# Cross-attention scores: the transposed scores computed a second time on TensorE, or turned by transposes after GpSimd has subtracted the row maximum

## The reference

```python
# L0 cross-attention, 16 heads of 8 features, query x, key and value ctx
q, k, v = proj(x, wq, bq), proj(ctx, wk, bk), proj(ctx, wv, bv)      # (B, 16, 256, 8)
scores = einsum('bhqd,bhkd->bhqk', q, k) / sqrt(8)
scores = where(mask[:, None], scores, -1e9)
attn = softmax(scores, axis=-1)
x = einsum('bhqk,bhkd->bhqd', attn, v)                               # then wo, bo
# L0 memory, ahead of it (w1, b1, w2, b2 updated by one gradient step)
out_mem = silu(x_in @ w1.T + b1) @ w2.T + b2
out = sigmoid(out_swa @ lin1.T) * out_swa + sigmoid(out_mem @ lin2.T) * out_mem
# L0 ffn, behind it: top 2 of 8 experts with a capacity; each token's row is scattered to its two experts
```

## Time and profile before

| | us |
|---|---|
| median of 3 runs (range) | 1086.91 (1083.47 to 1094.82) |
| the profiled execution | 1093.54 |
| its span, first to last instruction | 1091.5 |
| phase two: scores of step 0 begin | 342.64 |
| scores of steps 1, 2, 3 begin | 418.97, 497.19, 571.97 |
| last slots of step 3 written | 638.66 |

### The profile page before, as it was taken

The page is one execution under the profiler, slowest core; times in us unless marked ns, Lnnn a source line. Parts: engine busy times, 40 slices in busy tenths (PEclk is TensorE's granted clock), DMA queues, the critical chain, the costliest instruction groups (busy, mean ns, idle before and its releaser), DMA issues.

```text
span 1091.5 us, 14695 instructions
## 1 busy us (share of the span) xinstructions
PE 767.9 (70%) x4586; PEld 496.2 (45%) x4586; DVE 529.8 (49%) x1947; ACT 393.6 (36%) x924; POOL 158.9 (15%) x207
## 2 busy tenths in 40 slices
PE   5888787968453986977968919992664664664664
PEld 4445353544121663653645617882442442442442
DVE  4244253443333945936939321112556556556556
ACT  3514434252111542533532513330343343343343
POOL 9200000000101004013012040002040040040020
PEclk8798998999566997997977959997887887887886
DMA  7400000000106035054040011311000010010000
GB/s 220 144 7 13 1 19 0 19 0 0 53 22 103 2 54 93 0 64 81 9 64 20 2 43 37 91 49 44 20 25 6 29 24 5 29 24 5 10 0 10
DMA packets 49236, 39.37 MB, mean 36 GB/s; under 512 B 11234, under 2 KB 42658, under 8 KB 49188
## 3 DMA queue, kind: packets, MB, share of 16 engines
q1 hardware_dynamic: 47140, 34.62, 14.7%
q0 software_dynamic: 2048, 4.20, 1.4%
HBM read 27.20 MB, written 11.60 MB: 36 GB/s over the span
## 4 chain that ended last, share of the span: by engine, by line
PE 52%; DVE 20%; issue 11%; ACT 8%; DMA 5%; POOL 2%; SPq 2%; DVEq 0%; POOLq 0%; ACTq 0%
PE bank L1219 4%; DMA q_stack<-parts_dram 4%; PE bank L1208 4%; DVE R L2066 2%; PE bank L1102 2%; PE bank L960 2%; PE bank L1105 2%; PE bank L1104 2%; PE bank L1115 2%; PE bank L892 2%; PE bank L1022 2%; PE bank L1074 2%; PE bank L1029 2%; PE bank L1298 2%; PE bank L983 2%
## 5 line engine op out<-in xcount | busy, mean ns | idle before, releaser
L1815 DVE CUSTOM_DVE_ANT_0 bank<-bank,add_q 128x256 f32<-128x256 f32 x256 | 100.2, 458 | 45.2 <-PE bank L1074 29.6
L1509 ACT ACTIVATE pT<-bank 128x512 f32<-128x512 f32 x128 | 76.1, 597 | 73.7 <-PE bank L1105 71.4
L1074 PE MATMUL bank<-k_stack,q_stack 96*128 96x256 bf16 x256 | 52.1, 303 | 40.0 <-DMA q_stack<-parts_dram 34.8
L1238 PE MATMUL bank<-ident,X 128*128 128x128 f32 x48 | 14.3, 420 | 89.7 <-DVE X L1923 89.7
L1102 PE MATMUL bank<-q_stack,k_stack 96*128 96x256 bf16 x256 | 70.4, 275 | 2.1 <-DVE mx L1815 2.1
L1104 PE MATMUL bank<-add_k,ident_b 128*128 128x256 bf16 x256 | 70.8, 276 | 0.0
L1105 PE MATMUL bank<-neg_max,head_sel 96*128 96x256 bf16 x256 | 70.7, 276 | 0.0
L1298 PE MATMUL bank<-XT,kpad 128*128 128x256 f32 (+1 forms) x256 | 59.1, 364 | 3.3 <-DVE cT L2023 3.2
L2023 DVE TENSOR_TENSOR cT<-bank,decay 128x384 f32<-128x384 f32 x64 | 35.7, 558 | 43.8 <-POOL decay L847 43.3
L1298 PEld LDWEIGHTS bank<-XT,kpad 128*128 128x128 f32 x256 | 47.9, 210 | 16.5 <-DVE cT L2023 9.5
L1074 PEld LDWEIGHTS bank<-k_stack,q_stack 96*128 96x128 bf16 x256 | 25.3, 105 | 64.8 <-DMA q_stack<-parts_dram 31.8
(11 more groups left out here) (401 smaller groups left out, 1775.0 us busy)
## 6 DMA issues: line engine op xcount, KB each, us to landing
k_stack<-parts_dram SPq DMA_DIRECT2D x48, 64.0 KB
q_stack<-parts_dram SPq DMA_DIRECT2D x24, 128.0 KB, 10.1
expert_in<-no_rows SPq DMA_DIRECT2D x8, 324.0 KB, 3.9
rows<-expert_in SPq DMA_DIRECT2D x8, 324.0 KB
expert_out<-rows_y SPq DMA_DIRECT2D x8, 324.0 KB
moe_w<-in_L_ffn_w_dram SPq DMA_DIRECT2D x1, 2048.0 KB
parts_dram<-k_parts SPq DMA_DIRECT2D x4, 384.0 KB, 2.7
parts_dram<-q_parts SPq DMA_DIRECT2D x12, 128.0 KB, 1.7
```

Source lines behind the costliest of these rows:

```text
L1074: last = pe.matmul(q_bank(n)[:, c * S:(c + 1) * S], q_stack[:, h // 2, b * S + c * P:b * S + (c + 1) * P], k_stack[:, h // 2, h % 2, b * S ...
L1509: act.activation(pT[:, g % 2, j], k_bank(n)[:].rearrange("p (c q) -> p c q", c=QC), ACT.Exp).then_inc(exp_ready.sem, 1)
L1815: last = dve.tensor_tensor_reduce(sc, sc, add_q[:, b * QC + c, :], 1.0, 2.0 * NEG, ALU.add, ALU.max, mx[:, c, h:h + 1])
```

## The change

Each unit now has its scores on TensorE once. VectorE's reduction writes scores plus mask to an SBUF ring `shifted` (SLIDE = 4 units deep) and the two maxima to `mx`. GpSimd subtracts the maxima from the unit's 128x512 elements with one instruction (`s_shifted`). TensorE then transposes the four 128x128 blocks to PSUM (`scores_T`), and ScalarE takes the Exp as before. `scores` runs LEAD = 3 units in front. `mask_k`, `add_k`, `neg_max`, `maxima_T` and `negated` are gone. Silu is now half of z (1 + tanh(z/2)): Tanh and Identity on ScalarE, one VectorE instruction for the product, and the half goes into `memT`. `stack` is cut in `stack_k` and `stack_q`: for step 0 the K half is loaded ahead of `save_q`, and later steps wait for the last `s_ready` in place of `sT_ready`. The 8 scatters of a step move to the next step's units 2, 5, ..., 23. `outputs_T` of each batch is cut in two.

```diff
-        masks_loaded = signal("masks_loaded", 32)
+        masks_loaded = signal("masks_loaded", 16)
-        AHEAD = 14
+        LEAD = 3
+        SLIDE = 4
+        s_shifted = signal("s_shifted", XU)
...
+        z_of = (g2[:], memT[:])
+        mx = sb("mx", [P, SLIDE, QC], scope=stage)
+        shifted = sb("shifted", [P, SLIDE, QC, S], scope=stage)
...
+        pe_at = {3: 0, 5: 1, 7: 2, 9: 3, 11: 4, 13: 5, 15: 6, 18: 7, 23: 8, 25: 9}
+        act_at = {3: 0, 5: 1, 7: 2, 9: 3, 11: 4, 15: 6, 21: 7, 23: 8}
+        dve_at = {7: 0, 9: 1, 11: 2, 13: 3, 15: 4, 17: 5, 19: 6, 22: 7, 25: 8, 28: 9}
+        o_at = {21: 0, 23: 1}
...
             save_k(0)
+            stack_k(0)
             save_q(0)
-            stack(0)
+            stack_q(0)
...
-                    sp.wait_ge(*sT_ready.at(i))
-                    stack(i + 1)
+                    sp.wait_ge(*s_ready.at(i))
+                    stack_k(i + 1)
+                    stack_q(i + 1)
...
+            def scatter(i, n):
+
+                if n == 0:
+                    wait_apart(pool, passed, *slots_ready.at(i))
+                pool.indirect_dma_start(expert_in, bass.IndirectOffsetOnAxis(slot_i[:, n:n + 1], 0), Xm[:, n % NC, :], None).then_inc(scattered.sem, 16)
+
+            def heads(i, following):
+                for n in range(XU):
+                    wait_apart(pool, passed, *s_read.at(i, n + 1))
+                    pool.tensor_tensor(shifted[:, n % SLIDE], shifted[:, n % SLIDE], mx[:, n % SLIDE].unsqueeze(2).to_broadcast([P, QC, S]), ALU.subtract).then_inc(s_shifted.sem, 1)
+                    if following and n == 4:
+                        split_k(i + 1)
+                    if not is_first(i) and n % 3 == 2 and n // 3 < PAIRS:
+                        scatter(i - 1, n // 3)
                 if following:
+                    masks(i + 1)
...
-                def scores_k(n):
...
+                def scores_T(n):
+
+                    pe.wait_ge(*s_shifted.at(i, n + 1))
+                    if n >= 2:
+                        pe.wait_ge(*exp_ready.at(i, n - 1))
                     for c in range(QC):
+                        for k in range(QC):
+                            last = pe.transpose(sT_bank(n)[:, k * S + c * P:k * S + (c + 1) * P], shifted[:, n % SLIDE, c, k * P:(k + 1) * P], ident[:])
                     last.then_inc(sT_ready.sem, 1)
...
+                for n in range(LEAD):
+                    scores(n)
+                for n in range(XU):
+                    if n + LEAD < XU:
+                        scores(n + LEAD)
+                    scores_T(n)
+                    if n >= 5 and n % 4 == 1:
+                        values((n // 4 - 1) // G, (n // 4 - 1) % G)
+                    if n in o_at:
+                        outputs_T(0, o_at[n])
+                    if following and n == 1:
+                        keys(i + 1)
+                    if following and n in pe_at:
+                        head(i + 1, pe_at[n])
...
                     act.wait_ge(*zT_b.at(i, n + 1))
-                    act.activation(hT[:, n, 0:T], bank[1][:], ACT.Silu, bias=b1_new[:, n:n + 1]).then_inc(hT_b.sem, 1)
+                    if n >= 2:
+                        act.wait_ge(*hT_b.at(i, n - 1))
+                    act.activation(hT[:, n, 0:T], bank[1][:], ACT.Tanh, bias=b1_half[:, n:n + 1], scale=0.5)
+                    act.activation(z_of[n % 2], bank[1][:], ACT.Identity, bias=b1_new[:, n:n + 1]).then_inc(z_act.sem, 1)
...
+                if n < FC:
+                    dve.wait_ge(*z_act.at(i, n + 1))
+                    dve.scalar_tensor_tensor(hT[:, n, 0:T], hT[:, n, 0:T], 1.0, z_of[n % 2], ALU.add, ALU.mult).then_inc(hT_b.sem, 1)
...
                     wait_apart(dve, passed, *s_ready.at(i, n + 1))
+                    if n >= SLIDE:
+                        wait_apart(dve, passed, *sT_ready.at(i, n - SLIDE + 1))
                     for c in range(QC):
-                        last = dve.tensor_tensor_reduce(sc, sc, add_q[:, b * QC + c, :], 1.0,
-                                                        2.0 * NEG, ALU.add, ALU.max, mx[:, c, h:h + 1])
+                        last = dve.tensor_tensor_reduce(shifted[:, n % SLIDE, c, :], q_bank(n)[:, c * S:(c + 1) * S], add_q[:, b * QC + c, :], 1.0,
+                                                        2.0 * NEG, ALU.add, ALU.max, mx[:, n % SLIDE, c:c + 1])
```

More of the change, by code:

```diff
@@ L822, in _ @@
             pool.wait_ge(*slots_zero.at(0))
-            with pool.Fori(0, STEPS - 1) as i:
-                mix(i, True)
-            mix(STEPS - 1, False)
+            heads(0, True)
+            with pool.Fori(0, STEPS - 2) as i:
+                tail(i, True)
+                heads(i + 1, True)
+            tail(STEPS - 2, True)
+            heads(STEPS - 1, False)
+            tail(STEPS - 1, False)
+            for n in range(PAIRS):
+                scatter(STEPS - 1, n)
             pool.wait_ge(*scattered.at(STEPS - 1))
@@ L1139, in mix @@
-                pe.wait_ge(*slots_ready.before(i))
-                for g in range(NB * G + 1):
-                    for n in range(4 * g, min(4 * g + 4, XU)):
-                        scores_k(n)
-                        ahead = n + AHEAD
-                        if ahead < XU:
-                            scores_q(ahead)
-                        if ahead % 8 == 1 and ahead <= XU + 1:
-                            maxima_T(ahead // 8 - 1)
-                        if following and n in later:
-                            head(i + 1, later[n])
-                    if g == 6:
-                        outputs_T(0)
-                    if g > 0:
-                        values((g - 1) // G, (g - 1) % G)
@@ L1155, in mix @@
+                values(NB - 1, G - 1)
+                for c in range(QC):
+                    outputs_T(1, c)
                 if following:
-                    pe.wait_ge(*exp_ready.at(i))
+                    pe.wait_ge(*s_read.at(i))
+                    pe.wait_ge(*pv_ready.at(i))
                     values_of(i + 1)
@@ L1817, in mix @@
                     last.then_inc(s_read.sem, 1)
[L1819 to L1836 removed]
+                    if n - LEAD - 1 in o_at:
+                        outputs_of(0, o_at[n - LEAD - 1])
@@ L1837, in mix @@
+                    if following and n in dve_at:
+                        head(i + 1, dve_at[n], head_chain)
+                for c in range(QC):
+                    outputs_of(1, c)
                 if following:
@@ L2074, in _ @@
             head_chain = Chain(dve, dve_h, 0)
-            for n in range(4, 10):
+            for n in range(10):
                 head(0, n, head_chain)
```

166 lines of the change are left out of this document (52 added, 114 removed).

## The result

The changed kernel takes 1098.3 us (median of 20 runs, 1088.2 to 1106.8) against 1088.8 us (20 runs, 1081.6 to 1094.8): ratio 1.0074, 95% interval 1.0049 to 1.0100. Forecast were 1089.5 us and a range of 1068 to 1113. The time is inside, 8.8 us above the forecast; the medians differ by 9.5 us, where 2.6 were forecast.

What follows compares the result with a forecast made beforehand. TensorE was taken to bound the units, GpSimd to bound steps 1 to 3 after the change. The terms -6.2 - 4.9 + 18.5 + 4.6 - 7.4 - 0.4 - 1.6 = +2.6 us gave 1089.5 us, range 1068 to 1113.

Steps and rivals of the forecast that it cites:

- to the first reduction: Ahead of step 0: K's loads issued early save time, a second ScalarE instruction per MLP chunk costs 2.7 us; together -6.2 us.
- step 0: First of phase two's four steps: TensorE stays the bound, 47.9 us plus 2.1 of coupling, 50.0 us: -4.9.
- step 1, step 2: Middle steps of phase two: GpSimd becomes the bound with 51.7 us of work and 6.0 of stalls, 60.3 us: +9.2, +9.3.
- step 3: Last step of phase two: GpSimd's 48.6 us of work set it, with 1 us of stalls, 52.2 us: +4.6.
- turns to steps 1, 2: Between steps: stacks load earlier and VectorE's late start regains 3.7 of 7.4 us, twice: -7.4, plus 0.4 per tail.
- turn to step 3, last tail: Into step 3 the turn gains only 0.4 us; tail transposes cut in two gain 0.4 a step.
- The subtract: GpSimd's 32 subtracts of 128x512 a step: 1.20 us each from start to start, between 1.04 and 1.50.
- The stalls between engines: Waits within steps: 6.0 us in steps 1 and 2 (2.5 at unit 13, 2 low clock, 1.5 coupling), 2.1 in step 0.
- The fast subtract: Rival, chance 0.27: GpSimd isn't the wall, the subtract takes 1.04 us, stalls are 2 instead of 6 us; about 1070 us.
- The slow one: Rival, chance 0.14: the subtract takes 1.50 us and adds 29 us in steps 1 to 3, about 4 in step 0; 1122 us.
- TensorE's clock: Rival, chance 0.12: TensorE, partly idle in each unit, falls to its low clock, so a unit takes 1.8 us; 1112 us.
- The fourth rival: Chance 0.12: 9 VectorE instructions with two SBUF inputs keep GpSimd's subtracts waiting, 6.2 us a step in three steps; 1104 us.

Runs made afterwards that it cites:

- e11: Kernel before the change, with k_stack's first loads issued ahead of Q's first saves and VectorE's loop over the steps written out: 1073.5 us, ratio 0.9849.
- e3: Changed kernel with VectorE's split of Q moved from unit 28 to behind the last reduction: 1101.8 us, ratio 1.0103 to the kernel before.
- e7: Changed kernel with the split of Q behind the last reduction and k_stack's loads issued ahead of Q's saves: 1083.3 us, ratio 0.9948 to the kernel before.
- e5: Changed kernel without GpSimd's subtracts of the row maximum; transposes wait for the reductions instead: 1059.0 us, ratio 0.9718 to the kernel before.
- e9: As e7, with VectorE's loop over steps 0 to 2 written out: 1070.3 us, ratio 0.9836 to the kernel before.
- e10: As e11, with k_stack loaded in two halves, the first batch's as soon as unit 15 has used it: 1072.7 us, ratio 0.9856 to the kernel before.
- e1: Changed kernel with all 8 scatters of a step issued ahead of the next step's first subtract: 1104.0 us, ratio 1.0113 to the kernel before.
- e2: Changed kernel with 4 scatters ahead of the first subtract, the rest behind units 14, 17, 20, 23: 1096.9 us, ratio 1.0064 to the kernel before.
- e4: Changed kernel with TensorE's other blocks ahead of each unit's four transposes, not behind them: 1099.1 us, ratio 1.0090 to the kernel before.

## Why the prediction was right, and where it was wrong

| term | forecast | measured | |
|---|---|---|---|
| to the first reduction | -6.2 | -7.2 | right |
| step 0 | -4.9 | +3.2 | wrong sign |
| step 1, step 2 | +9.2, +9.3 | +9.3, +10.4 | right size, wrong sum |
| step 3 | +4.6 | -2.9 | wrong sign |
| turns to steps 1, 2 | -4.1, -4.1 | -4.3, -4.9 | right |
| turn to step 3, last tail | -0.8, -0.4 | +2.0, -1.0 | clock |
| sum in phase two | +2.6 | +4.6 | |

(The forecast's 0.4 us for each tail stands with its turn.) Outside phase two come the 3.0 us that the two turns of the second layer cost, a term that was put at nothing; the rest of the medians' 9.5 us is not accounted for. By the sign that the prediction itself named it was wrong, since the subtract is off its 1.20 us by more than 0.1. That the time came out near is in good part luck.

**Ahead of step 0.** The second instruction on ScalarE goes with 2.3 us (Q is saved 39.3 us behind the key projection, 37.0 before), forecast 2.7. From the save to the scores it takes 10.6 us; Q's half was put at 2 + 9. e11, without ScalarE's part, shows K first by itself: -10.8.

**The subtract** was taken at 1.20 us from start to start and runs at 1.0: the near end of the bracket, the flat row's 1.04. The per-partition broadcast and a different second operand cost nothing here. So the forecast had 6.4 us a step too much here.

**The stalls between engines** are the step that failed. I gave TensorE's bound in step 0 a coupling of 2.1 us and GpSimd's in steps 1 and 2 stalls of 6.0. With 1.0 us a subtract GpSimd's list in step 1 is 32.0 + 3.1 + 10.2 + 0.95 + 1.6 = 47.9 us, and the step took 60.4: 12.5 us of stalls. In step 0 TensorE was busy 48.0 us and idle 10.0. The forecast had it busy 51.5 - 7.0 = 44.5; its 47.9 holds 3.4 us of waits. A broken-up queue makes TensorE busier by itself: four transposes take 0.66 us after a wait and 0.44 in a row (the chain above). Steps 1 and 2 came out right because 6.4 too much stood against 6.5 too little. Scores, reduction, subtract and transposes form a ring with three units of lead, and each engine also carries blocks of 1 to 4 us (`split_k`, the MLP product, the split of Q). I priced one such meeting (2.5 us at unit 13) and rounded the rest. e3 and e7 measured another: the split of Q at unit 28 costs 2.4 to 3.5 us a step in e3 and 1.6 to 3.7 in e7; e5 measured what the subtract costs as a whole, 6.8 to 10.7. How the rest of the 12.5 us is shared out stays open.

**Step 3** has no such blocks, and there the forecast's picture holds (GpSimd's list sets the time): GpSimd's first subtract starts at 587.01 and its last ends at 629.36, 42.35 us, for 32 x 1.0 + 8 x 1.28 = 42.2. No stalls, and with 1.20 in place of 1.0 the forecast was 6.4 too high.

**The turns.** I took back 3.7 of VectorE's 7.4 us, so that 3.7 were left; measured are 3.37 and 3.29, with next to no DMA beside them (share 0.01). But the earlier trace rows did not mean what I took them for. In e11 taking those 7.4 us away gained nothing: before the change TensorE ran ahead in them. And the 0.57 us of the later loop, which I held for the price of a turn with idle queues, became 3.0 in the changed kernel with the queues idle. So full DMA engines only add to a delay that is there without them. The changed kernel has a lead of three units, so VectorE's start holds TensorE, 4.7 us at 421.78, and e9 gets 3 to 4 us a turn for removing it.

**The rivals.** The fast subtract came true without its time, since the stalls grew. The slow one is refuted. TensorE's clock fell in part: 0.93, 0.91 and 0.89 in steps 0 to 2 after 0.98 to 1.0, and TensorE is busy 48.5 us in step 1, not 48.1 - 7.0 = 41.1; in step 3 it rose from 0.83 to 0.93. By the Trainium skill (TensorE: Matmul & The Clock Gate, Part 4: PE-mode transpose) transposes don't hold the clock up; step 3, with four of them in every unit, was at 0.93 over 44.7 us, so here they do not prevent the high level beside matmuls. e10 and e11, without such transposes, have 0.92 to 0.98 in steps 0 to 2, so the transposes are not needed for a lower clock; no run separates them from TensorE's idle time. The clock goes with the turn to step 3 as well: 0.58 in it, and 21.6 us, where e1, e2 and e4 to e9 have 0.71 to 0.77 and 18.4 to 18.7 us. The fourth rival had the direction wrong: VectorE waits up to 2.3 us, while only 10 of the 128 subtracts took 1.3 to 1.5 us. The Trainium skill (SBUF — State Buffer, Who interferes with whom) says that the port pair which the two engines share is an exclusive lock, and that the order of issue decides who blocks. The trace agrees, and adds that a run of queued subtracts can go first together (2.95 us).
